# Softmax denominators of two attention layers: spread over the heads by transfers inside SBUF instead of by a TensorE product, in a four-layer graph network on one core

## The reference

```python
# layer 0: attention with 8 heads of 32, then layer norm
logits = einsum('bhqd,bhkd->bhqk', q, k) / sqrt(32) + log(clip(adj, 1e-8))[:, None]
out = einsum('bhqk,bhkd->bhqd', softmax(logits), v)
x = layer_norm(x + out @ Wo.T + bo)
# layers 1 and 3: additive attention over the features' projection
f = x @ W_fc; logits = f @ w_q + (f @ w_k).T + (1 - adj) * -1e9
x = softmax(leaky(logits)) @ f + x
# layer 2: 8 heads again, scores + a[i] + c[j] + log(adj + 1e-9), no output product
x = softmax(scores) @ v + x
```

## Time and profile before

| | |
|---|---|
| median of 3 runs | 1798.22 us (1797.73 to 1798.81) |
| the profiled execution, its span | 1798.2 us |
| PE busy | 1757.7 us, 98% of the span |
| DVE, ACT, POOL busy | 82%, 76%, 41% |
| groups, products of "wide" | 64, 128 |
| TensorE clock granted | 0.995 of full speed over the span |

### The profile page before, as it was taken

One profiled execution on the slowest core, in us unless ns is written; L12 is line 12 of the kernel. 1 busy time (PEld: TensorE's weight loads), 2 busy tenths in 40 slices (PEclk: granted clock), 3 DMA queues, 4 the chain that ended last, 5 costly groups with the idle time before them and its releaser, 6 DMA issues.

```text
span 1798.2 us, 68824 instructions
## 1 busy us (share of the span) xinstructions
PE 1757.7 (98%) x28155; PEld 1647.2 (92%) x28155; DVE 1475.6 (82%) x3361; ACT 1372.0 (76%) x3792; POOL 731.3 (41%) x797
## 2 busy tenths in 40 slices
PE   7999999999999999999999999999999999999997
PEld 6899999999999999999999999999999999999986
DVE  4688888888888888888888888888888888888875
ACT  3677787777787787787787787787787787787774
POOL 3343344343443343443443343343443443443421
PEclk8999999999999999999999999999999999999999
DMA  3101011011011011011011011011011011011100
GB/s 116 39 20 49 26 49 49 26 49 50 26 49 49 26 49 49 27 49 49 26 49 50 26 49 50 26 49 49 26 49 49 26 49 49 26 49 49 35 8 25
DMA packets 48261, 74.56 MB, mean 41 GB/s; under 512 B 5456, under 2 KB 21968, under 8 KB 47952
## 3 DMA queue, kind: packets, MB, share of 16 engines
q1 hardware_dynamic: 47376, 69.49, 12.1%
q10 hardware_dynamic: 576, 0.68, 0.1%
HBM read 53.37 MB, written 16.78 MB: 39 GB/s over the span
## 4 chain that ended last, share of the span: by engine, by line
PE 87%; ACT 3%; DMA 3%; DVE 3%; issue 2%; POOL 2%; SPq 0%; DVEq 0%; POOLq 0%; ACTq 0%
PE banks L1111 15%; PE banks L1176 14%; PE banks L1113 13%; PE banks L1112 13%; PE banks L1325 7%; PE banks L1220 6%; PE banks L1211 6%; DMA x_t<-x_t_dram 3%; PE banks L1199 2%; PE banks L1285 2%; PE banks L1225 2%; PE banks L1313 1%; PE banks L1319 1%; POOL weights_B L684 1%; PE banks L1279 1%
## 5 line engine op out<-in xcount | busy, mean ns | idle before, releaser
L684 POOL TENSOR_TENSOR weights_B<-weights_B,adj 128x512 f32<-128x512 f32 x64 | 113.0, 1766 | 299.1 <-ACT weights_B L765 299.1
L690 POOL TENSOR_TENSOR inv_parts_A<-inv_both_A,own 128x512 fp32r<-128x512 f32 x64 | 66.7, 1042 | 303.7 <-DVE inv_both_A L1035 303.7
L1000 DVE TENSOR_REDUCE least_cols_A<-banks 128x4 f32<-128x512 f32 x256 | 159.4, 684 | 33.8 <-PE banks L1176 33.7
L1000 DVE TENSOR_REDUCE least_B<-banks 128x4 f32<-128x512 f32 x256 | 172.6, 681 | 11.6 <-PE banks L1185 11.5
L1111 PE MATMUL banks<-w_hi_v,xt_hi 128*128 128x258 f32 (+1 forms) x512 | 157.3, 307 | 9.5 <-DVE pick L883 9.5
L1111 PE MATMUL banks<-w_hi_f,xt_hi 128*128 128x258 f32 x512 | 162.3, 317 | 2.3 <-DVE xt_lo L875 0.7
L839 ACT ACTIVATE fp<-banks 128x258 f32<-128x258 f32 x256 | 92.6, 390 | 89.1 <-PE banks L1113 89.1
L765 ACT ACTIVATE banks<-banks,v_B 128x256 f32<-128x256 f32 x384 | 153.4, 474 | 0.0
L1111 PE MATMUL banks<-xt_hi,w_hi_k 128*128 128x256 f32 x512 | 150.7, 294 | 0.3 <-DVE xt_lo L875 0.3
L1113 PE MATMUL banks<-w_lo_v,xt_hi 128*128 128x258 f32 (+1 forms) x512 | 145.1, 283 | 0.0
L1112 PE MATMUL banks<-w_hi_v,xt_lo 128*128 128x258 f32 (+1 forms) x512 | 145.0, 283 | 0.0
(11 more groups left out here) (192 smaller groups left out, 6172.0 us busy)
## 6 DMA issues: line engine op xcount, KB each, us to landing
x_t<-x_t_dram SPq DMA_DIRECT2D x64, 256.0 KB, 3.6
x_in<-x_dram SPq DMA_DIRECT2D x64, 256.0 KB, 3.6
out_dram<-x_out SPq DMA_DIRECT2D x64, 256.0 KB, 2.4
adj_t<-adj_t_dram SPq DMA_DIRECT2D x64, 128.0 KB, 3.4
adj<-adj_dram SPq DMA_DIRECT2D x64, 128.0 KB, 2.0
scratch<-weights_dram SPq DMA_DIRECT2D x9, 256.0 KB, 6.6
scratch<-weights_dram ACTq DMA_DIRECT2D x2, 256.0 KB, 4.3
out_bias<-L_gnn_bo_dram ACTq DMA_DIRECT2D x1, 128.0 KB, 7.8
```

The costliest lines, as they stand in the source:

```text
L684: pool.tensor_tensor(units, units, weight_of[where][:, G.four, :, :].unsqueeze(2).broadcast_to([P, GROUP, 2, P]), ALU.mult).then_inc(first ...
L1000: dve.tensor_reduce(to, bank[SCORE_BANKS[n]].rearrange("p (u m) -> p u m", u=UNITS), axis=AX.X, op=ALU.min).then_inc(maxed[where], 1)
```

## The change

PE's "wide" and POOL's product with "own" go, and with them the constants that they use. The sums are laid so that the rows of one head stand four apart. DVE only inverts, from the bank into a tile in SBUF (inv), and waits first until the former transfers from it have landed. A new step of SP, "spread", waits for that inverse and for the last reader of the former inv_wide, and issues four transfers from SBUF to SBUF, each of which copies every fourth row of inv over 32 partitions into one quarter of inv_wide (128x128, 64 KB). POOL's new step "scale" waits for the heads and for the four landings and multiplies inv_wide by the heads in place. ACT and DVE split, and DVE sums, from inv_wide.

SP's load becomes four steps with places of their own in the order. The orders of all engines, the first and last groups' too, are new, and the banks are given by a table (HOMES) instead of in turn. In a period, out_proj works on the same group as the scores of A (before, on the former one), and k0 and q0 one group ahead. The fillers are 162 instead of 143, all in the first and last groups.

The diff, with the tables cut to a line or two:

```diff
     "sync": [
-        (-1, "load", "", 0), (4, "store", "", 0)],
+        (-1, "load", "x_t", 0), (-1, "load", "adj_t", 0), (0, "load", "adj", 0), (3, "spread", "B", 0),
+        (6, "store", "", 0), (-1, "load", "x", 0), (0, "spread", "A", 0)],
...
             if name == "den":
-                return inv_split[where], g + 1
-            if name == "wide":
-                return (ot_lo_ready if where == "A" else x3_ready), g + 1
+                return inverted[where], g + 1
...
+                elif name == "load" and where == "adj":
                     G.wait_former(sp, one_minus, 1, 1)
                     sp.dma_start(adj[:, :], ins["adj"][G.no]).then_inc(adj_landed, 16)
+                elif name == "spread":
+                    sp.wait_ge(inverted[where], G.no + 1)
+                    G.wait_former(sp, ot_lo_ready if where == "A" else x3_ready, 1, 1)
+                    for u in range(UNITS):
+                        sp.dma_start(inv_wide[where][:, u, :],
+                                     inv[where][u:P:UNITS, :].unsqueeze(1).broadcast_to([HEAD_DIM, UNITS, P])
+                                     ).then_inc(inv_landed[where], 16)
...
-                pool.memset(sums[:, u, u * part:(u + 1) * part], 1.0).then_inc(const_ready, 1)
+                pool.memset(sums[:, u, u:HEAD_DIM:UNITS], 1.0).then_inc(const_ready, 1)
...
-                    elif name == "den":
-                        if G.no == 0:
-                            pool.wait_ge(setup_dve, dve_step["own", "", ""])
-                        pool.wait_ge(inv_split[where], G.no + 1)
-                        pool.tensor_tensor(inv_parts[where][:, :, :],
-                                           inv_both[where][:, :].unsqueeze(1).broadcast_to([P, UNITS, P]),
-                                           own[:, :].unsqueeze(2).broadcast_to([P, UNITS, P]), ALU.mult
-                                           ).then_inc(inv_placed[where], 1)
+                    elif name == "scale":
+                        pool.wait_ge(heads_ready[where], G.no + 1)
+                        pool.wait_ge(inv_landed[where], 16 * UNITS * (G.no + 1))
+                        flat = inv_wide[where][:, :, :].rearrange("p u n -> p (u n)")
+                        pool.tensor_tensor(flat, flat, heads[where][:, :, :].rearrange("p g d -> p (g d)"), ALU.mult
+                                           ).then_inc(ot_ready[where], 1)
...
-                        act.activation(ot_hi[:, :, :].rearrange("p g d -> p (g d)"), bank[BANK["wide", "A", 0]], ACT.Copy).then_inc(ot_hi_ready, 1)
+                        act.activation(ot_hi[:, :, :].rearrange("p g d -> p (g d)"),
+                                       inv_wide["A"][:, :, :].rearrange("p u n -> p (u n)"), ACT.Copy
+                                       ).then_inc(ot_hi_ready, 1)
...
                         dve.wait_ge(filled[b], fills.after(G, *key))
-                        dve.reciprocal(bank[b][:, 0:P], bank[b][:, 0:P]).then_inc(inverted[where], 1)
-                        dve.wait_ge(inverted[where], G.no + 1)
-                        dve.tensor_copy(inv_hi[where][:, :], bank[b][:, 0:P]).then_inc(inv_rounded[where], 1)
-                        dve.wait_ge(inv_rounded[where], G.no + 1)
-                        dve.scalar_tensor_tensor(inv_both[where][:, :], bank[b][:, 0:P], low_row[:, :],
-                                                 inv_hi[where][:, :].bitcast(F32), ALU.mult, ALU.subtract
-                                                 ).then_inc(inv_split[where], 1)
-                    elif name == "wide":
-                        dve.wait_ge(heads_ready[where], G.no + 1)
-                        dve.wait_ge(filled[b], fills.after(G, *key))
-                        dve.tensor_tensor(bank[b], bank[b],
-                                          heads[where][:, :, :].rearrange("p g d -> p (g d)"), ALU.mult
-                                          ).then_inc(ot_ready[where], 1)
+                        G.wait_former(dve, inv_landed[where], 16 * UNITS, 1)
+                        dve.reciprocal(inv[where][:, :], bank[b][:, 0:P]).then_inc(inverted[where], 1)
                     elif name == "sum":
...
-                                          bank[BANK["wide", "B", 0]].rearrange("p (g k n) -> p k g n", g=GROUP, k=KT),
+                                          inv_wide["B"][:, :, :].rearrange("p (g k) n -> p k g n", g=GROUP),
...
-            def wide(s, to):
-                return pe.matmul(to[:, :], spread[:, :, :].rearrange("p r d -> p (r d)"),
-                                 inv_parts[s][:, :, :].rearrange("p u n -> p (u n)"), start=True, stop=True)
```

More of the change, by code:

```diff
@@ new lines @@
+    "sync": [
+        (-1, "load", "adj_t", 0), (-1, "load", "x_t", 0), (-8, "store", "", 0), (-2, "load", "adj", 0),
+        (-5, "spread", "B", 0), (-7, "store", "", 0), (-2, "spread", "A", 0), (-1, "load", "x", 0),
+        (-4, "spread", "B", 0), (-6, "store", "", 0), (-1, "spread", "A", 0), (-5, "store", "", 0),
+        (-1, "load", "adj", 0), (-3, "spread", "B", 0), (-2, "spread", "B", 0), (-4, "store", "", 0),
+        (-1, "spread", "B", 0), (-3, "store", "", 0), (-2, "store", "", 0), (-1, "store", "", 0)],
@@ L254 @@
 }
 ENGINES = ("tensor", "vector", "scalar", "gpsimd", "sync")
-FILL_NAMES = ("scores", "again", "turn_max", "use", "den", "wide", "turn_x", "k", "q", "v", "fc", "mask", "turn_p",
+FILL_NAMES = ("scores", "again", "turn_max", "use", "den", "turn_x", "k", "q", "v", "fc", "mask", "turn_p",
               "mix", "turn_rows", "out_proj")
@@ L572, in load_weight, with step @@
                              ).then_inc(raw_landed[n], 16)
-            def step(name, G):
-                if name == "load":
+            def step(name, where, G):
+                if name == "load" and where == "x_t":
                     G.wait_former(sp, xt_ready["0"], 1, 1)
                     sp.dma_start(x_t[:, :], ins["x_t"][G.no]).then_inc(xt_landed, 16)
+                elif name == "load" and where == "adj_t":
                     G.wait_former(sp, adj0_ready, 1, 1)
```

161 lines of the change are left out of this document (66 added, 95 removed), and 365 rows, old and new, of tables (EARLY, FILLERS, HOMES, LATE).

## The result

The changed kernel took 1820.1 us (median of 4, 1816.2 to 1823.9) against 1798.0: a ratio of 1.0129, 95% interval 1.0106 to 1.0152. It is slower by 1.3%; forecast was 1762 and faster. The profiled execution has a span of 1814.4 us, 16.2 more than before.

The account below looks back on a forecast made before the run. The prediction took PE's row of matmuls, busy for 98% of the span, to bound the kernel. Its sum was 1798.2 - 29.5 - 9 - 8 + 9 + 1.5 = 1762 us, with a range of 1738 to 1800.

Parts of the forecast that it names:

- The wide products: On PE, 128 wide products go at 0.23 us each, all of it out of the time: -29.5 us.
- shorter joints of blocks: On PE, wide products' successors and one fewer three-pass block save 0.14 us in 64 periods: -9, bounds 0 and -20.
- Loads: On SP, x_t is issued some 7 us ahead, so PE's waits at the turn of x go: -8, bounds 0 and -11.6.
- The chain of stream B: From den B's start on PE (d), reciprocal, four transfers, POOL's product and DVE's sum end at d + 9.1 without collision.
- PE's demand: PE's turn_p 3, the end of stream B's chain, is due 12.1 us after den B starts.
- The collision: DVE's sum beside POOL's bias 0 is held up by 1.1 us, turn_p 3 0.15 late: +9, from 0 to +28.
- DVE does not hold PE, so this is worth nothing by itself: On DVE, losing the cast, the low part and the multiplication by the heads was counted at nothing.
- Ends: Last group's chain is uncovered at the tail: +1.5 (0 to +3); the start 0, with 4 us kept either way.
- D: Rival: the transfers land like bulk loads, in 3.6 us, making chains B and A late: about 1830 us; 15%.
- C: Rival: the last transfer lands after 2.8 to 3.2 us, with the collision on top: about 1785 us; 13%.
- B: Rival: the collision of DVE's sum with POOL's bias 0 is absorbed and costs PE nothing: 1753 us; 22%.
- E: Rival: PE's block exits cost like entries (-20 for -9), the start gains 4, no collision: 1738 us; 8%.

Follow-up runs that it names:

- c4: Changed kernel, groups 5 to 60: POOL's bias 0, turn_x 0, product A wait for DVE's sum, "less", maximum parts; qk 1 on POOL; spread B before load adj: 1761.9 us.
- c5: c4 without the wait of POOL's bias 0 for DVE's sum: 1790.7 us.
- qk_pool: Changed kernel, but in groups 10 to 53 POOL instead of DVE adds the bias of qk 1, ahead of its product of stream B: 1831.5 us.
- c2: Changed kernel with the waits of y_sum and y_parts and the edit of qk_pool together, groups 10 to 53: 1777.2 us.
- y_parts: Changed kernel, but in groups 10 to 53 POOL's product of stream A waits for DVE's parts of the maximum of B: 1805.8 us.
- y_sum: Changed kernel, but in groups 10 to 53 POOL's bias 0 waits for DVE's sum of stream B: 1793.0 us.
- less_sp: y_less with one more edit, SP issues spread B ahead of load adj: 1803.0 us.
- one_issue: Changed kernel, but each spread is one transfer of 256 KB instead of four of 64 KB, with wrong values for three units: 1780.3 us.
- y_less: Changed kernel, but in groups 10 to 53 POOL's turn_x 0 waits for DVE's "less" of the norm: 1838.6 us.

## Why the prediction was wrong, step by step

**PE's row.** The wide products: right. Most periods of c4 are 26.34 us long, most of those of before that had no wait 26.80: 0.46, which is what the two products alone were to give. With c4's mean, 26.37, it is 0.43. The term for the shorter joints of blocks (-9) came out at its lower bound, nothing: elsewhere the new row pays, as at turn_x 1 to turn_max A (0.49 for 0.44 on average).

**Loads.** Right in mechanism. ACT's wait for x_t is gone from the waits. The mean period of before exceeds the period without waits by 0.20, 12 us over 59 periods, most of it in ten periods of 27.4 to 28.6 in which PE waited for the turn of x; the prediction had 8.

**The chain of stream B.** Its times held, though not for the reasons given at its start. In the group of the rows above den B starts at 914.52, and the reciprocal, the load of adj and the four issues were:

```profile
916.37 0.94 DVE L1046 RECIPROCAL inv_B<-banks 128x128 f32<-128x128 f32 x1
...
916.79 0.33 SPq L619 DMA_DIRECT2D adj<-adj_dram  x1
917.33 2.47 SPq L624 DMA_DIRECT2D inv_wide_B<-inv_B  x4
```

The reciprocal, behind the held "less", ended at d + 2.8 and set the first issue; d + 2.1 was said, which is what it takes in c4, where "less" is free. The load came at d + 2.3 and not at d + 2.6. An issue took 0.62 instead of 0.47, so the last began at d + 4.7 (4.5 was said). Weigh A ended at d + 7.25 (7.1), the product at d + 8.5 (8.4), the sum at d + 10.3 (10.2). The landing was 2.0. The Trainium skill, "DMA: Bandwidth & Descriptors", section "Anatomy of one DMA", has its fit from transfers on GpSimd's path, and these were issued by SP; the estimate by it was 2.15, the trace's 2.0 decides, and neither moves the chain. PE's demand, d + 12.1, is met by the steps of c4, which add up to 12.07. What was mis-sized at its end is the wait: 0.15 was said, 0.29 measured at turn_p 3, and 0.62 in c5.

**The collision: the step that failed.** The prediction found the mechanism, weighed it against the rule of the Trainium skill, "SBUF — State Buffer", section "Who interferes with whom", and then applied it to one of the four steps that it hits. By the same section of the Trainium skill the order of issue decides who blocks, not the operation's shape. The rows agree: "less", on 128x2 elements, ended with POOL's operation on 128x512, 0.88 us late. "DVE does not hold PE, so this is worth nothing by itself" was the sentence that closed the search: it put the small steps that wait beside POOL, and PE behind them, at nothing. The +9 should have been the 0.93 to 0.97 a period of the table and of the mean over all 59 periods, +57: 0.35 at mask 1 and den A by qk (qk_pool, c2), 0.27 at turn_max B and 0.29 at turn_p 3. The last two are not owned by one step each. The parts' wait alone clears turn_max B (y_parts), the sum's clears it too and most of turn_p 3 (y_sum), and an earlier chain clears turn_p 3 although the sum is still held (less_sp, where "less" is free; one_issue). How the 0.29 divides between the sum and "less" is not shown.

The trace of before could have told. In its order POOL waited for a landing when "less" came, and DVE's small steps fell into POOL's pauses. But once "less" did not (min/median/max in ns, count 64):

```profile
L1077 DVE SCALAR_TENSOR_TENSOR less<-moments,rstd x64: 141/161/799, 47.2 to 1741.3; 128x2 f32<-128x2 f32 x64
```

One of 64 took 799 ns instead of 161, beside POOL's turn_x 0. In its steady periods the collision stood too, the other way round: in 57 of 64 groups DVE's turn_x, with two inputs in SBUF, began up to 0.03 us before POOL's weigh B and held it.

```profile
927.10 0.68 DVE L875 TENSOR_TENSOR xt_lo<-sum_t,xt_hi 128x512 fp32r<-128x512 f32 x1
...
927.11 1.82 POOL L684 TENSOR_TENSOR weights_B<-weights_B,adj 128x512 f32<-128x512 f32 x1 [4.50 <-ACT weights_B L765]
...
L684 POOL TENSOR_TENSOR weights_A<-weights_A,adj x64: 1278/1301/1318, 27.4 to 1721.6; 128x512 f32<-128x512 f32 x64
L684 POOL TENSOR_TENSOR weights_B<-weights_B,adj x64: 1287/1822/1835, 89.1 to 1775.3; 128x512 f32<-128x512 f32 x64
```

The same operation took 1.82 us there and 1.30 in weigh A, and PE's waits of before, from 140 to 1700 us, name it nowhere. In the new order weigh B takes 1.30, and it is DVE that is held.

**Ends.** +0.6 us instead of +1.5, and the first four periods are 4.7 us shorter, 0.7 beyond the 4 us that were kept for them. No run tells which part of the new start gives that.

**The balance.** Of the 59 periods behind the first four: -0.43 for the products, -0.20 for the loads and +0.97 of waits make +0.34 each, 20 us; with -4.7 and +0.6 the 16.2 us of the two spans.

**The rivals.** D, slower, was right in sign and wrong in mechanism: it needed a landing of 3.2 us, and the landing was 2.0. C needed the same, from 2.8 us on. B, the collision absorbed, fell with the rows of the sum, and E with it and with the joints. That c4 came out at the 1762 of the forecast is partly chance: the -9 of the joints did not come, and c4 has no +9 of a collision.

**What stays open.** one_issue and c4 were not combined, since the one transfer doesn't carry the right values. In the changed kernel the products inside PE's blocks follow each other at 119.2 ns on average, and at 118.5 before; no run tells why, and it is worth some 4 us at most.

## What to carry to other kernels

When a change gives POOL an operation that reads SBUF, or moves one, list every DVE instruction with both inputs in SBUF that can fall beside it, the tiny ones too, and ask who is queued behind each; compare the means of unchanged operations in both traces, since work that grows without being touched is the sign. The remedy can be a wait on the engine that has time: POOL was idle for more than half of the span, and three waits that keep it out of the way, with a 128x4 step moved and one order on SP turned, took 58 us off. Before such a wait is added, follow what the waiting engine releases through the other queues: y_less lost 18 us by a load on SP that stood ahead of the transfers.
